# Last block of a decoder: token rows gathered by a map instead of sorted in DRAM, results scattered straight to the output

## The reference

```python
def _L3_ffn_ref(hidden_states, Wr, br, Wg, Wu, Wd):   # D 256, D_FF 1024, N_EXPERTS 4
    x = hidden_states.reshape(-1, d)
    probs = jax.nn.softmax(x @ Wr + br, axis=-1)
    top_w, top_idx = jax.lax.top_k(probs, 1)
    g = jnp.einsum('td,edf->tef', x, Wg)
    u = jnp.einsum('td,edf->tef', x, Wu)
    y = jnp.einsum('tef,efd->ted', jax.nn.silu(g) * u, Wd)
    return jnp.take_along_axis(y, top_idx[:, :, None], axis=1)[:, 0] * top_w

x = x + _L3_ffn_ref(_layernorm(x, axis=-1), L3_ffn_Wr, ..., L3_ffn_Wd)
return x
```

## Time and profile before

| | us |
|---|---|
| median of three timed runs (2314.5 to 2316.04) | 2314.92 |
| the profiled execution | 2308.51 |
| its span | 2306.7 |
| TensorE busy in the span | 1889.3 (82%) |
| VectorE busy in the span | 1283.2 (56%) |
| GpSimd busy in the span | 261.5 (11%) |

### The profile page before, as it was taken

One profiled execution on the slowest core, in us unless ns is written; L12 is line 12 of the kernel. 1 busy time (PEld: TensorE's weight loads), 2 busy tenths in 40 slices (PEclk: granted clock), 3 DMA queues, 4 the chain that ended last, 5 costly groups with the idle time before them and its releaser, 6 DMA issues.

```text
span 2306.7 us, 25589 instructions
## 1 busy us (share of the span) xinstructions
PE 1889.3 (82%) x9040; PEld 1204.9 (52%) x9040; DVE 1283.2 (56%) x2981; ACT 770.5 (33%) x1813; POOL 261.5 (11%) x248
## 2 busy tenths in 40 slices
PE   6675667788449699999756858999998999996795
PEld 3441223545335366666544636555555577785453
DVE  5648998654863444444586586333334666664122
ACT  4125445104122133333421412333333455552110
POOL 3611000000114100000120110000000222210001
PEclk9796877999759799999866979999999899997898
DMA  3010000000442200000000032000002000003001
GB/s 143 1 55 0 0 0 20 28 1 2 187 163 89 101 1 1 1 1 1 37 0 1 2 147 96 33 1 1 1 1 111 1 1 1 1 1 140 32 23 46
DMA packets 19501, 84.72 MB, mean 37 GB/s; under 512 B 2513, under 2 KB 12500, under 8 KB 15280
## 3 DMA queue, kind: packets, MB, share of 16 engines
q1 hardware_dynamic: 17072, 76.94, 8.5%
q0 software_dynamic: 2304, 6.15, 0.8%
HBM read 73.01 MB, written 10.22 MB: 36 GB/s over the span
## 4 chain that ended last, share of the span: by engine, by line
PE 69%; DVE 17%; issue 6%; POOL 3%; ACT 2%; DMA 1%; POOLq 0%; SPq 0%; DVEq 0%; ACTq 0%
PE bank L136 56%; PE bank L141 8%; PE bank L3317 3%; DVE space L793 2%; PE bank L3339 2%; DVE space L782 1%; DVE space L2879 1%; DVE space L1357 1%; DVE space L178 1%; DMA space<-in_L_attn 1%; POOL space L623 1%; POOL space L637 0%; ACT space L2934 0%; DVE space L1519 0%; POOLq L3787 0%
## 5 line engine op out<-in xcount | busy, mean ns | idle before, releaser
L136 PE MATMUL bank<-space 128*128 128x256 f32 (+15 forms) x6722 | 1456.8, 425 | 96.7 <-DVE space L2879 19.0
L136 PEld LDWEIGHTS bank<-space 128*128 128x128 f32 (+7 forms) x6722 | 890.2, 182 | 613.2 <-issue 392.8
L141 PE MATMUL bank<-consts,space 128*128 128x128 f32 (+1 forms) x1610 | 260.0, 306 | 223.2 <-DVE space L189 67.2
L141 PEld LDWEIGHTS bank<-consts,space 128*128 128x128 f32 (+1 forms) x1610 | 206.2, 155 | 292.9 <-issue 168.2
L136 PE MATMUL bank<-space,consts 128*128 128x512 f32 (+2 forms) x148 | 91.1, 754 | 56.0 <-DVE space L788 48.8
L197 POOL TENSOR_TENSOR space<-space,consts 128x4 f32<-128x4 f32 x22 | 24.9, 1132 | 634.9 <-DVE space L184 634.9
L2569 POOL TENSOR_TENSOR space<-space,consts 128x4 f32<-128x4 f32 x64 | 68.6, 1071 | 220.7 <-DVE space L2500 220.7
L2318 DVE TENSOR_REDUCE space<-bank 128x2 f32<-128x512 f32 x64 | 44.0, 688 | 87.0 <-PE bank L136 86.8
L2364 ACT ACTIVATE space<-bank,space 128x256 f32<-128x256 f32 x128 | 59.5, 470 | 95.7 <-DVE space L2318 95.7
L2492 DVE TENSOR_REDUCE space<-bank 128x2 f32<-128x512 f32 x64 | 44.2, 691 | 71.1 <-PE bank L136 71.1
L136 PEld LDWEIGHTS bank<-space,consts 128*128 128x128 f32 x148 | 31.9, 238 | 99.0 <-DVE space L788 70.2
(11 more groups left out here) (333 smaller groups left out, 1976.2 us busy)
## 6 DMA issues: line engine op xcount, KB each, us to landing
space<-in_L_ffn SPq DMA_DIRECT2D x13, 2048.0 KB, 12.4
space<-in_L_attn SPq DMA_DIRECT2D x10, 2048.0 KB, 12.9
space<-in_L_xattn SPq DMA_DIRECT2D x4, 2048.0 KB, 9.7
expert_results<-space SPq DMA_DIRECT2D x16, 128.0 KB, 3.7
space<-expert_results SPq DMA_DIRECT2D x8, 256.0 KB, 4.6
space<-in_L_xattn SPq DMA_DIRECT2D x1, 1919.0 KB, 19.4
space<-in_L_xattn SPq DMA_DIRECT2D x1, 1536.0 KB, 6.2
sorted_rows<-space SPq DMA_DIRECT2D x11, 128.0 KB, 16.3
```

The costliest lines, as they stand in the source:

```text
L136: return self.nc.tensor.matmul(out, lhsT, rhs, start=first, stop=last, skip_group_check=True)
L141: return self.nc.tensor.transpose(out, src, eye)
```

## The change

The list in DRAM goes, and with it the zeros, the clears, the eight scatters, SP's loads and stores, the list of results, the eight gathers, the eight updates of x, and the eight stores of x to the output. In their place:

- ScalarE issues four transfers that write a table `top_tokens` of 1024 rows with 520 numbers: the normalized token (in two halves, behind ScalarE's copies of the transposed tokens), x itself (behind the exponential), and the token's eight sorted probabilities (behind the maxima, `weighed`).
- `find` on VectorE, with 8 bf16 products on TensorE, makes from the places a map `take` (which token stands in each row; token 0 where none does) and a map `put` (the same, with a number out of range where none does).
- GpSimd gathers each block's rows from the table by `take`, four ahead. A row's buffer is now kept until the block's result is taken, since VectorE forms result * weight + x from it (in place of the copy of L3417). GpSimd scatters the result to the output by `put`; rows out of range are left out. There are five result buffers instead of three.
- TensorE's router products wait for the first half of the transposed tokens, and for the second half ahead of the fifth tile.
- The small weights gain the constants for `find`.

```diff
-        self.rows_dram = c.nc.dram_tensor("sorted_rows", (N * P, D), F32).ap()
-        self.results_dram = c.nc.dram_tensor("sorted_results", (N * P, D), F32).ap()
-        self.zero = c.sb(D)
+        self.table = c.nc.dram_tensor("top_tokens", (TOK, self.ROW), F32).ap()
+        self.out = c.out.rearrange("b s d -> (b s) d")
...
+        self.past, self.slot, self.of_row = c.sb(NT, N + 1), c.sb(2, NT), c.sb(NT, N)
+        self.marks, self.spots = c.sb(NT, 2, N, dt=BF16), c.sb(NT, P, dt=BF16)
+        self.map, self.token, self.gone = c.sb(2, N), c.sb(2, N), c.sb(N)
+        self.take, self.put = c.sb(N, dt=U32), c.sb(N, dt=U32)
...
+        self.rows_in, self.rowsT = c.bufs(4, self.ROW), c.bufs(3, DC, P)
+        self.hs, self.hTs, self.results = c.bufs(5, HALF), c.bufs(4, 2, HALF), c.bufs(5, D)
...
+        self.stored = [c.moves((N - k + 4) // 5) for k in range(5)]
+        self.tabled = c.moves(4)
...
         self.x_turned.tensor(e, self.norm.s.normed)
-        self.x_turned.wait(e)
         e.wait_ge(*self.ld.all)
         for i in range(NT):
+            if i % 4 == 0:
+                self.x_turned.wait(e, i // 4)
...
-        e.wait_ge(*s.place_ready.all)
+        e.wait_ge(*s.spotted.all)
+        for i in range(NT):
+            done = c.mm(bk[6][:, 0:2 * N], self.spots[:, i, :], flat(self.marks[:, i, :, :]), i == 0, i == NT - 1)
+        done.then_inc(*s.mapped.one)
         e.wait_ge(*s.at_ready.all)
         e.wait_ge(*self.late.all)
...
+            last = nc.vector.max(self.best[:, i, :], self.pr[:, i, :])
+        last.then_inc(*s.weighed.one)
+        e.wait_ge(*s.weighed.all)
...
-        nc.vector.tensor_copy(self.place_i, self.place).then_inc(*s.place_ready.one)
+
+    def find(self, e):
+
+        c, w, s, bk, nc, N = self.c, self.w, self.s, self.c.banks, self.c.nc, TOP_BLOCKS
+        m = self.map
+        nc.vector.tensor_tensor(self.past, spread(self.place, N + 1), repeat(w["edges"], NT), ALU.is_ge).then_inc(*c.v.next())
+        e.wait_ge(*c.v.so_far)
+        nc.vector.tensor_reduce(self.slot[:, 0, :], self.past[:, :, 1:N + 1], AX.X, ALU.add).then_inc(*c.v.next())
+        nc.vector.tensor_tensor(self.of_row, self.past[:, :, 0:N], self.past[:, :, 1:N + 1],
+                                ALU.subtract).then_inc(*c.v.next())
+        e.wait_ge(*c.v.so_far)
+        nc.vector.scalar_tensor_tensor(out=self.slot[:, 1, :], in0=self.slot[:, 0, :], scalar=-float(P), in1=self.place,
+                                       op0=ALU.mult, op1=ALU.add).then_inc(*c.v.next())
+        nc.vector.tensor_scalar(self.marks[:, :, 0, :], self.of_row, w["names"][:, 0:1], None, ALU.mult)
+        nc.vector.tensor_tensor(self.marks[:, :, 1, :], self.of_row, spread(w["tiles"], N), ALU.mult)
+        e.wait_ge(*c.v.so_far)
+        nc.vector.tensor_tensor(self.spots, repeat(c_bf(w["slots"]), NT), spread(self.slot[:, 1, :], P),
+                                ALU.is_equal).then_inc(*s.spotted.one)
+        e.wait_ge(*s.mapped.all)
+        nc.vector.tensor_copy(flat(m), bk[6][:, 0:2 * N]).then_inc(*c.v.next())
+        e.wait_ge(*c.v.so_far)
+        nc.vector.scalar_tensor_tensor(out=self.token[:, 0, :], in0=m[:, 1, :], scalar=float(P), in1=m[:, 0, :],
+                                       op0=ALU.mult, op1=ALU.add).then_inc(*c.v.next())
+        nc.vector.tensor_scalar(self.gone, m[:, 1, :], 0.0, 1.0e6, ALU.is_equal, ALU.mult).then_inc(*c.v.next())
+        e.wait_ge(*c.v.so_far)
+        nc.vector.tensor_scalar(self.token[:, 1, :], self.token[:, 0, :], -float(P), 0.0, ALU.add,
+                                ALU.max).then_inc(*c.v.next())
+        nc.vector.scalar_tensor_tensor(out=self.gone, in0=self.token[:, 0, :], scalar=-float(P), in1=self.gone,
+                                       op0=ALU.add, op1=ALU.add).then_inc(*c.v.next())
+        e.wait_ge(*c.v.so_far)
+        nc.vector.tensor_copy(self.take, self.token[:, 1, :]).then_inc(*s.take_ready.one)
+        nc.vector.tensor_copy(self.put, self.gone).then_inc(*s.put_ready.one)
...
-        nc.vector.memset(self.zero, 0.0).then_inc(*s.zeroed.one)
         nc.vector.memset(flat(self.pr), -1.0).then_inc(*c.v.next())
...
         self.route(e)
+        self.find(e)
...
-                if j >= 3:
-                    e.wait_ge(*self.stored[j % 3](j // 3))
+                row = self.rows_in[j % 4]
+                if j >= 5:
+                    e.wait_ge(*self.stored[j % 5](j // 5))
                 e.wait_ge(*s.out_mm(j + 1))
-                nc.vector.tensor_copy(self.results[j % 3], bk[7][:, 0:D]).then_inc(*s.out_taken.one)
+                nc.vector.scalar_tensor_tensor(out=self.results[j % 5], in0=bk[7][:, 0:D], scalar=row[:, 2 * D:2 * D + 1],
+                                               in1=row[:, D:2 * D], op0=ALU.mult, op1=ALU.add).then_inc(*s.out_taken.one)
...
-        for i in range(NT):
-            e.wait_ge(*self.got[i].all)
-            nc.vector.scalar_tensor_tensor(out=c.x[:, i, :], in0=self.xn[:, i, :], scalar=self.best[:, i, 0:1],
-                                           in1=c.x[:, i, :], op0=ALU.mult, op1=ALU.add)
...
+        table = self.table.rearrange("(t p) d -> p t d", p=P)
         self.x_turned.scalar(e)
+        for g in range(2):
+            e.wait_ge(*self.norm.s.normed(4 * g + 4))
+            e.dma_start(table[:, 4 * g:4 * g + 4, 0:D], self.xn[:, 4 * g:4 * g + 4, :]).then_inc(*self.tabled.one)
         p4 = self.pr[:, :, 0:E]
         e.wait_ge(*s.centred.all)
         nc.scalar.activation(p4, p4, ACT.Exp).then_inc(*s.exps.one)
+        e.dma_start(table[:, :, D:2 * D], c.x).then_inc(*self.tabled.one)
+        e.wait_ge(*s.weighed.all)
+        e.dma_start(table[:, :, 2 * D:2 * D + 8], self.best).then_inc(*self.tabled.one)
...
-        e.wait_ge(*self.cleared.all)
-        e.wait_ge(*s.place_ready.all)
-        e.wait_ge(*self.norm.s.normed.all)
-        for i in range(NT):
-            nc.gpsimd.indirect_dma_start(
-                self.rows_dram, bass.IndirectOffsetOnAxis(ap=self.place_i[:, i:i + 1], axis=0), self.xn[:, i, :], None,
-                bounds_check=N * P - 1, oob_is_err=True).then_inc(*self.scattered.one)
+        e.wait_ge(*self.tabled.all)
+        e.wait_ge(*s.take_ready.all)
+        for t in range(N + 4):
+            if t < N:
+                if t >= 4:
+                    e.wait_ge(*s.out_taken(t - 3))
+                nc.gpsimd.indirect_dma_start(
+                    self.rows_in[t % 4], None, self.table, bass.IndirectOffsetOnAxis(ap=self.take[:, t:t + 1], axis=0),
+                    bounds_check=TOK - 1, oob_is_err=True).then_inc(*self.arrived[t % 4].one)
+            if t >= 4:
+                j = t - 4
+                if j == 0:
+                    e.wait_ge(*s.put_ready.all)
+                e.wait_ge(*s.out_taken(j + 1))
+                nc.gpsimd.indirect_dma_start(
+                    self.out, bass.IndirectOffsetOnAxis(ap=self.put[:, j:j + 1], axis=0), self.results[j % 5], None,
+                    bounds_check=TOK - 1, oob_is_err=False).then_inc(*self.stored[j % 5].one)
         for signal in self.stored:
             e.wait_ge(*signal.all)
-        for i in range(NT):
-            nc.gpsimd.indirect_dma_start(
-                self.xn[:, i, :], None, self.results_dram, bass.IndirectOffsetOnAxis(ap=self.place_i[:, i:i + 1], axis=0),
-                bounds_check=N * P - 1, oob_is_err=True).then_inc(*self.got[i].one)
-
-    def sync(self, e):
-        s, N = self.s, TOP_BLOCKS
-        e.wait_ge(*s.zeroed.all)
-        for j in range(N):
-            e.dma_start(self.rows_dram[j * P:(j + 1) * P, :], self.zero).then_inc(*self.cleared.one)
-        e.wait_ge(*self.scattered.all)
-        for t in range(N + 3):
-            if t < N:
-                if t >= 4:
-                    e.wait_ge(*s.row_turned(t - 3))
-                e.dma_start(self.rows_in[t % 4], self.rows_dram[t * P:(t + 1) * P, :]).then_inc(*self.arrived[t % 4].one)
-            if t >= 3:
-                j = t - 3
-                e.wait_ge(*s.out_taken(j + 1))
-                e.dma_start(self.results_dram[j * P:(j + 1) * P, :], self.results[j % 3]).then_inc(
-                    *self.stored[j % 3].one)
...
+        "slots": halves(every(i.astype(np.float32))), "tiles": every(np.arange(1, NT + 1, dtype=np.float32)),
+        "names": i[:, None].astype(np.float32), "edges": every(np.arange(TOP_BLOCKS + 1, dtype=np.float32) * P),
...
-            for i in range(NT):
-                e.dma_start(od[:, i, :], c.x[:, i, :]).then_inc(*stored.one)
-            e.wait_ge(*stored.all)
+            if not stages[-1][1].stores:
+                for i in range(NT):
+                    e.dma_start(od[:, i, :], c.x[:, i, :]).then_inc(*stored.one)
+                e.wait_ge(*stored.all)
```

16 lines of the change are left out of this document (7 added, 9 removed).

## The result

| us | before | changed |
|---|---|---|
| median of four timed runs each | 2315.48 (2314.5 to 2317.99) | 2291.9 (2288.34 to 2295.51) |
| ratio, 95% interval | | 0.9901 [0.9884, 0.9917] |
| profiled execution, its span | 2308.51, 2306.7 | 2295.51, 2292.0 |

Faster by 23.6 us, and the median is 0.5 us above the forecast of 2291.4. The profiled execution of the changed kernel was the slowest of its four, so its span is only 14.7 us shorter. To compare the stage that was changed, I count from the start of the previous stage's last update of x ("t0"): A is from there to the loop's first transpose, B from there to the start of VectorE's last operation on a result, C the rest of the span.

A forecast was written before the change was run, and what follows sets the result against it. TensorE bounds the loop; two idle stretches, before the first row and after the last result, were to shrink by 7.5 + 16.0 = 23.5 us, taking 2314.92 to 2291.4 us; range 2287 to 2298.5.

The forecast's parts named there:

- GpSimd's pacing: Rival in the loop: gather, wait for the result and scatter share one queue, TensorE waits every row; 2320 us, chance 0.04.
- the held ScalarE: Rival at the front: issuing two table stores blocks ScalarE's queue ahead of the exponential, costing 2 us; 2293.5 us, chance 0.05.
- The memset: Front, head of VectorE's work: the memset of zero rows goes, gain 0.27 us.
- Halves: Front, router's products: they wait for one half of the transposed tokens at a time, gain 0.73 us, or 0.
- Find: Front: making the address map on VectorE and TensorE takes 3.95 us, with 3.0 and 4.9 as ends.
- The gather: Front: the first gather of 2,080-byte rows takes 3.17 us from GpSimd's start to use, ends 2.8 and 4.1.
- First row: End of the front: the loop's first row is there at 2136.47 instead of 2143.94, 7.5 us earlier.
- The table: Front, ScalarE's queue: four table stores land by 2127 to 2132.6, hidden behind routing and find, costing nothing.
- the late table: Rival at the front: the table's fourth store lands after the addresses, costing up to 4 us; about 2294 us, chance 0.10.
- The loop: Loop over blocks: multiply-add instead of copy, a gather and a scatter a round on GpSimd; nothing charged.
- fourth rival: The front gives nothing: the loop doesn't wait for the first row, or half-clock matmuls lose the gain; 2299 us, chance 0.05.
- The end: After the last result: multiply-add, scatter and GpSimd's drain take 5.3 us instead of 21.31, gain 16.0, ends 14.7 and 17.3.

The follow-up runs named there:

- halves_only: The kernel before with only the router's products waiting for the transposed tokens by halves; one execution took 2306.39 us, the stage 202.57 us against 203.29.
- front_only: The kernel before with the change's front alone (table of tokens only, gathers by map), old end kept; median 2300.92 us against 2315.22, ratio 0.9937.
- two_gathers: The changed kernel with the table split into tokens and the rest, two gathers a block; the stage took 181.08 us against 180.40.

## Why the prediction was right, step by step

- *What bounds the kernel* was read rightly: the idle stretch between the places and the first row, and the end behind the last result. The loop stayed TensorE's, its clock 1.00, and GpSimd's pacing and the held ScalarE did not happen (0.96 us for two issues, where SP had taken 15.1 for eleven).
- *The memset*, 0.27: VectorE's first statistics (L178) are on the chain 0.98 us behind t0 instead of 1.25.
- *Halves*, 0.73: 1.06 at the places in halves_only, because the products' own piece of the chain is 0.34 shorter too, which the prediction did not have; 0.98 in A, 0.72 in the stage's sum.
- *Find*, 3.95: 2136.26 to 2140.06 is 3.80. *To GpSimd*, 0.96: 0.91. Both were priced by the mixture block's rows of the same form.
- *The gather*, 3.17: 3.52, the largest miss of the front. The step that failed is the price of the second kilobyte: I took the rate of the full DMA engines (0.37 us for 135 KB), and the two kernels differ by 0.57, some 235 GB/s. The base of 2.80 was 0.15 short as well. The Trainium skill (DMA: Bandwidth & Descriptors, Anatomy of one DMA: some 2.0 us and the bytes at 436 GB/s) gives estimates of 2.30 and 2.61 us for the two sizes; 2.95 and 3.52 were measured.
- *First row* 7.5 us earlier: 7.64 in A. Two misses of the same size cancelled, the products' 0.34 that nobody had in the sum and the gather's 0.35; that part of the agreement is luck.
- *The table*: hidden, as forecast, and the landing (2137.9, or 2129.7 counted as in the execution before, 8.2 us less) lies inside my 2127 to 2132.6. But the reasoning was better than its margin in one point and worse in another: the tokens' stores were to be done by 2121 to 2125 and x's by 2127, and by the old count they landed at 2125.8 and 2128.8, and the engines were full until 2128. The weights' store of small rows landed 0.9 us behind x's, near the low end of "between nothing and 5.6 us". In the eleven kernels with this store it landed 0.9 to 2.5 us behind the last large transfer, where 1024 kilobyte rows take 3.0 us at 344 GB/s. So it did not cost more per row than those, as the rival needed; what read-modify-write costs, which the prediction cites for it, no run isolates. And "its cover is the 10 us that routing and find take" is no measure of the slack, which was 2.1 us. I gave the late table 0.10; for something that 2.1 us decide that was fair, and no comfort.
- *The loop*, nothing: B 0.40 longer. The first 16 matmuls took 8.96 us instead of 8.56, at half clock for the first 3.7 us instead of 2.9. My fourth rival, that half clock eats what the front wins, was right in kind and small in size. The term was put at nothing, and it is 0.40. Over the kernels without added matmuls B mostly grows as A shrinks: 141.3 at A 40.7, 141.5 at 39.7, 141.6 at 36.8, 141.7 to 141.8 at 33, 141.7 (front_only) and 142.1 (two_gathers) at 32.4.
- *The end*, 5.3: 5.66. The drain ended 3.97 us behind the scatter's start, where I had taken the 3.74 of a drain in the earlier trace rows; the rest is the tail of 0.4 instead of 0.3. The gain is 15.65 instead of 16.0. What I did not know is why: the drain pays for all 22 indirect DMAs.
- *Sum*: 22.9 in the stage against 23.5. The front is 0.2 better than forecast, the loop 0.4 and the end 0.35 worse. The medians differ by 23.6, and the 0.7 between these is less than the unchanged stages vary. That the time came out within 0.5 us of the forecast is partly luck, as the 14.3 us of front_only show; that the stage did rests on the terms above.

## What to carry to other kernels

Price a replaced transfer by a row of the same form in the same trace, and judge the result by a segment that starts where the changed code starts, when the rest of the program varies by more than the terms you argue about. Of a transfer that is hidden, work out the slack in microseconds (landing against the moment it is needed), with all the bytes that are under way beside it; that number says how much of the next improvement will be seen. Ahead of an end that waits for a queue's drain, spend a drain where the engine is idle.
